# Perceiver layer on one core: in the token attention, ScalarE takes the exponentials ahead of two row copies

## The reference, cut to what matters

```
q = X @ w_q.T + b_q
v = jnp.einsum('bld,lp->bdp', X, Wp)
k = jnp.einsum('blc,lp->bcp', q, Wp)
attn = jnp.einsum('bhld,bhdp->bhlp', qh, kh)
attn = jax.nn.softmax(attn.astype(jnp.float32), axis=-1).astype(attn.dtype)
out = jnp.einsum('bhlp,bhpd->bhld', attn, vh)
out = out @ w_out.T + b_out
...
x = x + _L0_attn_ref(_layernorm(x, axis=-1), ...)
x = x + _L0_ffn_ref(_layernorm(x, axis=-1), ...)
```

## Time and profile before

| | |
|---|---|
| median of three executions | 544.65 us (543.02 to 545.02) |
| profiled execution, first to last instruction | 541.7 us (the record holds no other time of it) |
| TensorE busy | 497.2 us, 92% |
| VectorE busy | 399.4 us, 74% |
| ScalarE busy | 200.2 us, 37% |
| GpSimd busy | 198.7 us, 37% |
| mean granted clock of TensorE | 0.979 |

### The profile page before, as it was taken

The page is one execution under the profiler, slowest core; times in us unless marked ns, Lnnn a source line. Parts: engine busy times, 40 slices in busy tenths (PEclk is TensorE's granted clock), DMA queues, the critical chain, the costliest instruction groups (busy, mean ns, idle before and its releaser), DMA issues.

```text
span 541.7 us, 14453 instructions
## 1 busy us (share of the span) xinstructions
PE 497.2 (92%) x5012; PEld 347.4 (64%) x5013; DVE 399.4 (74%) x1068; ACT 200.2 (37%) x617; POOL 198.7 (37%) x314
## 2 busy tenths in 40 slices
PE   7998999999999999999999998999979979999960
PEld 7665666656666666666656566666735568888840
DVE  3699799999899999999562678788775325555545
ACT  2343422432332233333311566655431035555500
POOL 4000413112222221122222666665776615665620
PEclk9999999999999999999999999999998989999995
DMA  7999679786988988884017999310122235554249
GB/s 278 349 354 273 204 237 321 269 215 201 304 279 291 300 291 287 282 274 139 21 44 212 278 299 310 117 51 2 50 88 80 96 109 158 162 146 123 76 163 302
DMA packets 67348, 108.83 MB, mean 201 GB/s; under 512 B 8115, under 2 KB 49125, under 8 KB 67304
## 3 DMA queue, kind: packets, MB, share of 16 engines
q1 hardware_dynamic: 60888, 97.83, 58.0%
q0 software_dynamic: 3792, 8.43, 4.5%
q10 hardware_dynamic: 2624, 1.97, 1.2%
HBM read 85.31 MB, written 24.85 MB: 203 GB/s over the span
## 4 chain that ended last, share of the span: by engine, by line
PE 70%; DMA 9%; DVE 6%; POOL 5%; issue 4%; ACT 4%; SPq 1%; ACTq 0%; POOLq 0%; DVEq 0%
PE banks L1109 15%; PE banks L1133 15%; PE banks L1515 8%; DMA ring<-in_ctx_dram 4%; POOL rows_by_expert L727 4%; PE banks L1527 4%; PE banks L1121 3%; DVE ctxT L1637 3%; PE banks L1146 3%; PE banks L1068 2%; PE banks L1509 2%; PE banks L1249 2%; PE banks L1242 2%; PE banks L1265 2%; DMA xn_all<-expert_out 2%
## 5 line engine op out<-in xcount | busy, mean ns | idle before, releaser
L1637 DVE STREAM_TRANSPOSE ctxT<-ring 128x832 f32<-128x832 f32 x128 | 121.7, 1007 | 4.7 <-DMA ring<-in_ctx_dram 4.7
L1109 PE MATMUL banks<-ctxT,qT_all 32*64 32x416 f32 (+2 forms) x2048 | 93.9, 498 | 1.9 <-issue 1.2
L1133 PE MATMUL banks<-ring,prob 128*64 128x256 f32 (+1 forms) x832 | 93.6, 381 | 0.7 <-ACT prob L839 0.7
L1133 PEld LDWEIGHTS banks<-ring,prob 128*64 128x64 f32 (+1 forms) x832 | 58.6, 137 | 31.5 <-issue 4.2
L1109 PEld LDWEIGHTS banks<-ctxT,qT_all 32*64 32x64 f32 x2048 | 56.9, 131 | 30.6 <-issue 13.4
L638 POOL TENSOR_TENSOR var<-mv,eps 128x1 f32<-128x1 f32 x32 | 6.3, 196 | 166.8 <-DVE mv L1682 114.8
L761 POOL DMA_INDIRECT expert_out<-prob,dest x47 | 46.2, 984 | 40.5 <-DVE prob L2098 26.6
L852 ACT ACTIVATE prob<-banks,negmax 128x416 f32<-128x416 f32 (+2 forms) x80 | 41.1, 531 | 30.2 <-DVE negmax L1659 30.2
L1515 PE MATMUL banks<-ring,ctxT 128*128 x188 | 50.2, 391 | 0.0
L674 POOL TENSOR_TENSOR ctxT<-ctxT,k_mask 128x1088 f32<-128x1088 f32 x16 | 33.1, 2069 | 30.8 <-ACT ctxT L930 30.8
L839 ACT COPY prob<-banks 128x512 f32<-128x512 f32 x64 | 27.5, 514 | 38.1 <-PE banks L1121 38.1
(11 more groups left out here) (269 smaller groups left out, 939.4 us busy)
## 6 DMA issues: line engine op xcount, KB each, us to landing
ring<-in_ctx_dram SPq DMA_DIRECT2D x48, 1024.0 KB
qT_all<-q_by_pair SPq DMA_DIRECT2D x56, 128.0 KB, 9.0
rows_by_expert<-blank SPq DMA_DIRECT2D x8, 774.0 KB, 6.8
ctxT<-rows_by_expert SPq DMA_DIRECT2D x47, 129.0 KB, 2.1
mid<-stage SPq DMA_DIRECT2D x31, 128.0 KB, 2.3
ring<-in_ctx_dram SPq DMA_DIRECT2D x16, 130.0 KB
ctxT<-mid SPq DMA_DIRECT2D x16, 128.0 KB, 3.9
qT_all<-mid SPq DMA_DIRECT2D x16, 128.0 KB, 4.6
```

Of the source, the lines that this page charges most:

```text
L1109: last = pe.matmul(S[a][64 * b:64 * b + 64, 0:KW[a]], q_rep[mine, r, c, 64 * b:64 * b + 64], ctxT[mine, c, b, 0:KW[a]], start=c == 0, stop ...
L1133: last = pe.matmul(U[64 * b:64 * b + 64, 0:D], probT[0:rows, k, 64 * b:64 * b + 64], ring[0:rows, r, b, k, :], start=k == 0, stop=k == KT)
L1637: dve.transpose(ctxT[:, c].rearrange("p b (k j) -> p (b k) j", j=Q), ring[:, r].rearrange("p b k c -> p (b k) c")[:, :, columns(c):columns ...
```

## The change

In `turn` on ScalarE, the exponential (with its wait for `shifted_ready`) moves from behind the two copies of `n2_now` to the place ahead of them. Nothing is added or removed; in turns without the copies nothing moves.

```
                     act.wait_ge(n2T_done, i - 3)
                     for dh in range(DH):
                         act.copy(n2T[dh][:, bass.ds((i - 4) * P, P)], bank[6][:, dh * P:dh * P + P]).then_inc(n2T_copied, 1)
-                    act.copy(n2_first[:, bass.ds(i - 4, 1), 0:D].squeeze(1), n2_now).then_inc(n2a_ready, 1)
-                    act.copy(n2_second[:, bass.ds(i - 4, 1), 0:D].squeeze(1), n2_now).then_inc(n2b_ready, 1)
                 if back1:
                     act.wait_ge(shifted_ready, i)
                     act.activation(attn, attn, ACT.Exp).then_inc(exp2_done, 1)
+                if back4:
+                    act.copy(n2_first[:, bass.ds(i - 4, 1), 0:D].squeeze(1), n2_now).then_inc(n2a_ready, 1)
+                    act.copy(n2_second[:, bass.ds(i - 4, 1), 0:D].squeeze(1), n2_now).then_inc(n2b_ready, 1)
```

## The result

| | before | changed |
|---|---|---|
| median of four executions each, same chip | 544.01 us | 539.9 us (537.0 to 540.22) |
| ratio, estimated over the executions (the medians alone give 0.9924) | | 0.9914, 95% interval 0.9886 to 0.9941 |
| profiled execution, first to last instruction | 541.7 us | 538.5 us |
| first exponential of the attention, in that record | 298.14 us | 300.01 us |
| from the first exponential to the sixteenth | 87.19 us | 81.73 us |

The forecast of the median was 539.3 us; that of the profiled span, 536.3, is missed by 2.2. The kernel before has here one execution more than the three that the forecast started from, and a median of 544.01 instead of 544.65.

What follows compares the result with a forecast made beforehand. TensorE's attention chain passes through ScalarE's two copies before the exponential. Shifts of 4.2 (turns 4 to 10), 4.54 after turn 12, 4.96 after 14 and 5.4 after 15, rounded to 5.3, gave 544.65 - 5.3 = 539.3 us; 8-in-10 range 537.3 to 542.4.

Steps and rivals of the forecast that it cites:

- the exponential takes L935's slot: ScalarE, regular attention turns: the exponential starts where the first copy stood, 0.61 us earlier; 0.60 gained per turn.
- What was feared of the exponential behind L934: ScalarE, regular turns: at worst the exponential waits for L934's full end, some 0.1 us per turn, 0.7 over seven.
- The slack of 0.55 and 0.49: TensorE, regular turns: spare us left at L1249 (needing L910) and L1281 (needing L917) after the copies move behind.
- VectorE's wait before L1794: VectorE, regular turns: of 0.91 us waiting per turn 0.61 goes, leaving about 0.30 before this instruction, L1793 before.
- turn 11's gain is lost: VectorE has no wait in turn 12, so turn 11's 0.60 us does not reach its next subtraction.
- in such a turn L1273 follows 0.48 behind its start, not 0.59: TensorE, turns 12 to 14: with ScalarE idle before the exponential, its response is 0.10 us shorter in each.
- Given back later: After the attention: scatter or experts wait for something unshifted, 543.5 to 544.6 us; chance 0.13 together with "No effect".
- allowed for this clock in one direction: Start of the experts: TensorE's half-clock period might shorten, saving up to 1.6 us; luckier-clock case 537.3 to 537.9, chance 0.03.
- The second bound: Attention turns: GpSimd or VectorE closes the gap before the 0.30 slack, losing 2.1 of 5.3 us: 541.5; chance 0.10.
- No effect: Attention turns: the exponential waits for VectorE's subtraction anyway, 544 us; chance 0.13 together with "Given back later".
- Slower: Displaced copies ahead of L910 and L913 hold TensorE; at 1.1 us per copy, 548.6 us; chance 0.04.
- The case that was given 0.70: The forecast as worked out: 539.3 us, likeliest range 537.7 to 540.5, chance 0.70.

Runs made afterwards that it cites:

- the half change: Changed kernel with only n2_second's copy behind the exponential, n2_first's staying ahead of it: 542.07 us, ratio 0.9943.
- the runs with more copies: Changed kernel with two or four additional unread copies behind the exponential, ahead of the displaced two: 541.56 us (two) and 548.84 us (four).
- the kernel with one wait less: Changed kernel without TensorE's wait for n2T_copied ahead of L1274: 540.1 us, ratio 0.9902.
- two more copies ahead: Kernel before the change, with two additional unread copies of n2_now ahead of the exponential: 553.16 us, ratio 1.0135.
- the spread: Changed kernel with VectorE's running sum moved from turn 12 to 13, and the places' sum and conversion from 14 to 15: 541.03 us, ratio 0.9927.
- four more copies: Changed kernel with four additional unread copies behind the exponential, ahead of the displaced two: 548.84 us, ratio 1.0049.

## Why the prediction was right, and by how much

**Regular turns.** The step "the exponential takes L935's slot" held to 0.01: 5.41 against 5.41, and the half change gave half. Seven turns were summed to 4.2; they gave 4.13, since turns 4 and 5 gained 0.54 and 0.55 instead of 0.60: there the subtraction ends behind the slot, as the prediction said itself. What was feared of the exponential behind L934 (up to 0.1 per turn) is not there: it follows the subtraction by 0.06. The slack of 0.55 and 0.49 that was worked out for L1250 and L1282 reads 0.54 and 0.53 in the timeline, but the runs with more copies show that 0.44 of it can be used, for TensorE's response to each copy belongs to it. VectorE's wait before L1794 stayed at 0.39 rather than 0.30, and its wait before L1821 went entirely.

**Turns 12 to 14.** The mechanism held: all three exponentials wait for the subtraction, turn 11's gain is lost, and so is turn 13's. The sum missed here. The step that failed is the one by which "in such a turn L1273 follows 0.48 behind its start, not 0.59", for ScalarE would be idle before it. The earlier trace rows had shown an idle ScalarE and a missing second wait at once, since turn 2 has no copies of L934; the prediction chose the first, and the kernel with one wait less shows that it was the second. The result alone says so too: in turns 12 to 14 ScalarE is idle, both waits stand, and the distance is 0.57. The step was counted at 0.10 in turn 12 and 0.10 in turn 14.

**The shift carried out of the attention**, as L1274 against the first exponential (for turn 16, the end of its subtraction):

| after turn | forecast | measured |
|---|---|---|
| 10 | 4.2 | 4.13 |
| 12 | 4.54 | 4.38 |
| 14 | 4.96 | 4.71 |
| 15 | 5.4 | 5.13 |
| 16 | 5.4 | 5.15 |

**Where 2.2 us of the profiled span are.** The forecast was 536.3 and the record says 538.5. Of this 0.25 is the above. 1.87 is the first exponential's later start in this record, ahead of anything changed; in the record of the same kernel taken again it lies 0.50 earlier than in the one of before. So the span of one record was no measure of a change of 5 us to within 2, and this was not in the prediction's bounds at all. The rest, 0.1, hides two larger terms that cancel.

**Behind the attention.** From the sixteenth subtraction to the end it is 156.7 us before and 156.8 changed, so nothing was given back on balance; "Given back later" is refuted. But inside it the experts' first matmul comes 50.3 us behind that subtraction instead of 51.2 (432.00 and 436.22 by the records), and the clock takes it back. The stretch of the earlier trace rows in the changed kernel's record, then in the one of before, a little wider cut (columns as there):

```profile
431.50:438.00 6.50, 5.87 (x18) 4.53 (x19) 1.08 (x9) 1.87 (x6) 0.00 (x0) 0.50 0.45 118
438.00:443.00 5.00, 5.00 (x29) 4.39 (x28) 2.21 (x13) 2.63 (x9) 1.57 (x2) 0.99 0.30 80
```

```profile
436.00:441.00 5.00, 4.68 (x16) 3.48 (x17) 0.84 (x7) 1.40 (x4) 0.00 (x0) 0.66 0.42 115
441.00:446.00 5.00, 5.00 (x30) 4.39 (x29) 2.26 (x13) 2.78 (x11) 1.39 (x2) 1.00 0.36 106
```

The lower level of 1.2 GHz lasted 3.4 us before (5 us at a mean of 0.66) and at least 6.5 us after. Just ahead of it TensorE had stood idle for the experts' rows, 3.69 us before and 2.94 changed. The forecast had allowed for this clock in one direction, up to 1.6 better; it came in the other, by about 1.0. Ten records can be compared (in two others TensorE also waits for ScalarE there, 1.3 and 1.8 us, and in that of two more copies ahead the experts begin 10 us later). Those whose mean clock from 425 to 450 us is 0.93 take 105.0 to 105.8 us from the experts' first matmul to the end (six, the one of before among them), and those with 0.86 take 106.2 to 106.9 (four, both of the changed kernel among them). Whether the change itself has a part in it is not shown; the mean granted clock of whole executions differs within one kernel, from 0.976 to 0.985 in the changed one as in the one before.

**The other rivals.** "The second bound" did not come in the regular turns: `normed` (L903) waits for GpSimd's L692, 1.6 us in seven turns, and TensorE shows no idle time for it there. The port that it spoke of is real, as the earlier trace rows had shown, and costs more than the 0.5 allowed for (1.22 in the spread), but only in a turn that pairs a VectorE instruction of two SBUF inputs with GpSimd. "No effect" is refuted by 5.41. "Slower" has its place right, at L1281, and its threshold nearly: it needs 1.1 more on ScalarE by the prediction and 0.44 + 0.61 = 1.05 by the runs; four more copies, 1.22, bring it about.

The case that was given 0.70 came, and "faster", under 541.9, with it. The forecast of 539.3 stands 0.6 under the 539.9 and inside the measurement's own spread, and that it is so near is in part luck. The gain was forecast as 5.3 and is 4.1 by the two medians; the median before had come out 0.64 lower, which hides half of the difference. By the ratio's interval the gain is 3.2 to 6.2, so the median cannot tell 5.3 from the 5.15 of the stretch; the changed kernel taken again, beside another 545.11, gives 5.3.

## What to carry to other kernels

In a software-pipelined turn, list for each engine what stands ahead of the instruction that another engine waits for, and put behind it whatever has a late reader; the gain per turn is the displaced work, up to the gap that the waiting engine shows, and the room behind is read from the slack of what is queued there. Before you sum it over the turns, look for the turns in which another engine has no wait at all: there the gain of the turn before is lost. Judge a change in one stage by the stretch between two of its own events, which here repeated within 0.01 us for one kernel while the start of the stage moved by 2.4 us. When you read the room of a queued instruction from a timeline, take off the waiting engine's response, here 0.05 to 0.10 us.

## What the runs showed of the hardware

- A second semaphore wait ahead of a TensorE instruction, long satisfied, lengthened the response to ScalarE's exponential from 0.48 (0.50 in regular turns) to 0.57 (0.59). That the cost lies in its being an instruction of its own in the queue is likely (eleven fewer), but was not tried otherwise.
- VectorE's running sum with two SBUF inputs took 0.79 where it was issued ahead of GpSimd's instruction, 1.64 and 2.01 where it was issued behind GpSimd's L674 of 2.07, each time ending about 0.64 behind it; L674 lost nothing.
- ScalarE's exponential, its two copies and L910 start 0.33, 0.30 and 0.31 apart, while their records say 0.45, 0.41 and 0.42: what a displaced copy costs is the distance of the starts, 0.3, and not its 0.42.
- TensorE starts its queries 0.05 to 0.06 behind the recorded end of the ScalarE copy that it waits for, and its weighted sum 0.10 behind.
- The level of 1.2 GHz at the start of the experts lasts about 3.4 us before and at least 6.5 us in the changed kernel; the records at the two mean clocks differ by about 1 us of 540.
